# Wider recurrence products for the gates g, i and f, and q and k projections called by halves

## The reference, cut to what matters

```python
def step(carry, inp):
    h, c, n = carry
    i_t = sigmoid(xi_t + h @ Wih)
    f_t = sigmoid(xf_t + h @ Wfh)
    g_t = tanh(xg_t + h @ Wgh)
    o_t = sigmoid(xo_t + h @ Woh)
    c_t = f_t * c + i_t * g_t
    n_t = f_t * n + i_t * exp(g_t @ Weg + beg)
    h_t = o_t * (c_t / n_t)
...
qkv = x @ Wqkv          # per layer, q and k of 16 heads x 64
```

## Time and profile before

| | |
|---|---|
| median of 3 runs | 5900.19 us (5891.82 to 5912.33) |
| the profiled execution's own time | 5933.24 us |
| its span from first to last instruction | 5931.4 us |
| mean granted TensorE clock over the span | 0.895 |
| PE (matmul) busy | 5537.3 us, 93% |
| PEld (weight load) busy | 3641.9 us, 61% |
| DVE (VectorE) busy | 4517.5 us, 76% |
| ACT (ScalarE) busy | 2971.1 us, 50% |
| POOL (GpSimd) busy | 2368.6 us, 40% |

### The profile page before, as it was taken

One profiled execution on the slowest core, in us unless ns is written; L12 is line 12 of the kernel. 1 busy time (PEld: TensorE's weight loads), 2 busy tenths in 40 slices (PEclk: granted clock), 3 DMA queues, 4 the chain that ended last, 5 costly groups with the idle time before them and its releaser, 6 DMA issues. The chain is left out here.

```text
span 5931.4 us, 142026 instructions
## 1 busy us (share of the span) xinstructions
PE 5537.3 (93%) x51507; PEld 3641.9 (61%) x51508; DVE 4517.5 (76%) x15132; ACT 2971.1 (50%) x7179; POOL 2368.6 (40%) x2224
## 2 busy tenths in 40 slices
PE   4999999999999999999999999999998999998777
PEld 2555555666677666666666666667666555554353
DVE  4888888777777777787677677677777888886737
ACT  2666666444455454444444444454444666665030
POOL 3666665333333333333233333333333666664000
PEclk9999999888889899888788788898888999999888
DMA  3111110000000000000000000000001000000000
GB/s 111 32 35 35 35 39 21 17 16 14 16 14 16 14 25 5 25 12 12 5 25 5 24 5 25 5 25 5 25 5 30 28 28 28 28 11 1 10 2 17
DMA packets 106581, 123.24 MB, mean 21 GB/s; under 512 B 55014, under 2 KB 87480, under 8 KB 98872
## 3 DMA queue, kind: packets, MB, share of 16 engines
q1 hardware_dynamic: 105788, 114.34, 6.2%
q10 hardware_dynamic: 124, 0.03, 0.0%
HBM read 91.28 MB, written 23.07 MB: 19 GB/s over the span
## 5 line engine op out<-in xcount | busy, mean ns | idle before, releaser
L1593 POOL TENSOR_TENSOR t<-t 128x1024 f32<-128x1024 f32 x192 | 453.4, 2362 | 1264.3 <-DVE t L942 1264.3
L518 PE MATMUL banks<-h,lent 128*128 128x2 f32 x6144 | 937.3, 269 | 0.5 <-DVE banks L891 0.4
L594 PE MATMUL banks<-Wvo,xq 128*32 128x512 f32 x6144 | 891.7, 654 | 6.0 <-ACT Vw L1296 2.0
L518 PEld LDWEIGHTS banks<-h,lent 128*128 128x128 f32 x6144 | 884.6, 217 | 1.6 <-DVE banks L891 0.6
L1586 POOL TENSOR_TENSOR t<-t 128x1024 f32<-128x1024 f32 x192 | 453.9, 2364 | 868.5 <-DVE t L942 868.5
L515 PEld LDWEIGHTS banks<-h,lent 128*128 128x128 f32 x2048 | 373.1, 216 | 541.2 <-DVE h L923 403.6
L1219 ACT ACTIVATE ge<-banks 128x2 f32<-128x2 f32 x1024 | 176.1, 172 | 1001.6 <-PE banks L515 997.3
L910 DVE TENSOR_SCALAR banks<-es 128x6 f32<-128x6 f32 x1024 | 170.3, 166 | 634.5 <-ACT es L1228 625.3
L1296 ACT COPY Vw<-banks 128x512 f32<-128x512 f32 x768 | 450.9, 587 | 370.8 <-PE banks L594 364.7
L937 DVE TENSOR_TENSOR t<-banks,rl 128x1024 f32<-128x1024 f32 x384 | 468.5, 1220 | 106.9 <-ACT sq L1251 64.3
L1601 POOL TENSOR_TENSOR t<-t,rnorm 128x1024 f32<-128x1024 f32 x192 | 365.9, 1906 | 388.6 <-DVE rnorm L111 381.8
(11 more groups left out here) (314 smaller groups left out, 10820.1 us busy)
## 6 DMA issues: line engine op xcount, KB each, us to landing
Wqk<-in_L_ffn_Wqkv SPq DMA_DIRECT2D x24, 1024.0 KB, 5.0
Wvo<-wvo_kept SPq DMA_DIRECT2D x18, 1024.0 KB, 5.0
rl<-tables SPq DMA_DIRECT2D x24, 512.0 KB, 3.7
W<-in_L_ffn_W SPq DMA_DIRECT2D x24, 341.0 KB
tables<-tables SPq DMA_DIRECT2D x6, 1024.0 KB
wvo_kept<-Wvo SPq DMA_DIRECT2D x6, 1024.0 KB, 5.2
v_kept<-Vw SPq DMA_DIRECT2D x24, 256.0 KB, 2.5
Vw<-v_kept SPq DMA_DIRECT2D x24, 256.0 KB, 2.6
```

Source lines behind the costliest of these rows:

```text
L518: last = pe.matmul(sb[:, to + gate * B:to + (gate + 1) * B], c.Wg[:, gate + 1, 1, :], h, start=False, stop=True, skip_group_check=True)
L594: last = pe.matmul(vp[WIN * hq:WIN * hq + WIN, :], c.xq[n % 4][:, WIN * w:WIN * w + WIN], c.Wvo[stage % 2][:, hq, :], start=True, stop=True)
L1593: pool.tensor_tensor(t1, t1, t2[:, :], ALU.add).then_inc(s.k_sum, 1)
```

## The change

Three things change.

1. Each of the gates g, i and f takes h not once (2 columns) but repeated up to 32 times (64 columns). The last two columns of the output are the ones that the token needs; the others fall on the columns of tokens that have been used already, going backwards in the ring at its pitch of 4 or 6 columns, so nothing reads them. How often h is repeated follows from how many places lie behind the token in the bank: at the first token of a ring's first half 25 times for g and 17 for i and f, and 32 times from the eighth and the sixteenth token on and in the whole second half. To make this room, the rings begin at column 96 (`INPUTS`), and VectorE's scratch moves from column 384 to 480. Gate o and the product with Weg keep their two columns.
2. `project_q` and `project_k` do one half of the product at a call, and are called twice in a row at the same places; each half raises the semaphore. Nothing stands between the two calls.
3. The waits for `q_done` and `k_done` count twice as far.

```diff
+INPUTS, BROAD = 96, 32
-SUMS, SIGMAS, IG, RN = 384, 392, 400, 408
+SUMS, SIGMAS, IG, RN = 480, 488, 496, 504
...
+    def gate_of(k):
+        j, r = divmod(k, AHEAD)
+        return INPUTS + j % 2 * 4 * AHEAD + 4 * r, min(BROAD, r + 1 + INPUTS // 4 + j % 2 * AHEAD)
+
+    def sigmoids_of(k):
+        j, r = divmod(k, AHEAD)
+        return INPUTS + j % 2 * 6 * AHEAD + 6 * r, min(BROAD, r + 1 + INPUTS // 6 + j % 2 * AHEAD)
+
+    def ending(out, at, wide, n, part):
+        return out[:, at + wide - n * wide:at + wide].rearrange("p (n c) -> p n c", c=wide)[:, :, part * B:(part + 1) * B]
+
     def recur(k):
...
-        h = c.h[t % 2][:, :, i - 1] if i else c.h[1 - t % 2][:, :, P - 1]
-        at, to = j % 2 * 4 * AHEAD + 4 * r, j % 2 * 6 * AHEAD + 6 * r
+        h = (c.h[t % 2][:, :, i - 1] if i else c.h[1 - t % 2][:, :, P - 1]).unsqueeze(1)
+        (at, m), (to, n) = gate_of(k), sigmoids_of(k)
...
-        pe.matmul(ge[:, at:at + B], c.Wg[:, 0, 1, :], h, start=False, stop=True, skip_group_check=True).then_inc(s.g_done, 1)
+        pe.matmul(ending(ge, at, 4, m, 0), c.Wg[:, 0, 1, :], h.to_broadcast([P, m, B]), start=False, stop=True, skip_group_check=True).then_inc(s.g_done, 1)
...
         for gate in range(3):
-            last = pe.matmul(sb[:, to + gate * B:to + (gate + 1) * B], c.Wg[:, gate + 1, 1, :], h, start=False, stop=True, skip_group_check=True)
+            wide = n if gate < 2 else 1
+            last = pe.matmul(ending(sb, to, 6, wide, gate), c.Wg[:, gate + 1, 1, :], h.to_broadcast([P, wide, B]), start=False, stop=True, skip_group_check=True)
...
-    def project_k(n):
+    def project_k(n, h):
...
-        claim("qk", s.k_prod, 2 * n + 2)
-        for h in range(2):
-            last = pe.matmul(qk[h], c.xq[n % 4][:, :], c.Wqk[stage % 2][:, INNER + h * 512:INNER + (h + 1) * 512], start=True, stop=True)
-        last.then_inc(s.k_done, 1)
+        if h == 0:
+            claim("qk", s.k_prod, 2 * n + 2)
+        pe.matmul(qk[h], c.xq[n % 4][:, :], c.Wqk[stage % 2][:, INNER + h * 512:INNER + (h + 1) * 512], start=True, stop=True).then_inc(s.k_done, 1)
...
-        project_k(i - 2)
+        project_k(i - 2, 0)
+        project_k(i - 2, 1)
...
-        act.wait_ge(s.k_done, n + 1)
+        act.wait_ge(s.k_done, 2 * n + 2)
...
-                sp.wait_ge(s.k_done, 2 * SPAN * (stage - 1))
+                sp.wait_ge(s.k_done, 4 * SPAN * (stage - 1))
```

More of the change, by code:

```diff
@@ L521, in recur, with project_q @@
         pe.matmul(ge[:, at + B:at + 2 * B], c.Weg[:, :], c.ge[:, 0, :], start=False, stop=True, skip_group_check=True).then_inc(s.e_done, 1)
-    def project_q(n):
+    def project_q(n, h):
         if not tile_ok(n):
@@ L526, in project_q @@
         stage = place(n)[0]
-        pe.wait_ge(s.weights_in[stage % 2], 16 * (stage // 2 + 1))
-        pe.wait_ge(s.xq_ready, SHIFTS[n])
-        claim("qk", s.q_prod, 2 * n + 2)
-        for h in range(2):
-            last = pe.matmul(qk[h], c.xq[n % 4][:, :], c.Wqk[stage % 2][:, h * 512:(h + 1) * 512], start=True, stop=True)
-        last.then_inc(s.q_done, 1)
-    def project_k(n):
+        if h == 0:
+            pe.wait_ge(s.weights_in[stage % 2], 16 * (stage // 2 + 1))
+            pe.wait_ge(s.xq_ready, SHIFTS[n])
+            claim("qk", s.q_prod, 2 * n + 2)
+        pe.matmul(qk[h], c.xq[n % 4][:, :], c.Wqk[stage % 2][:, h * 512:(h + 1) * 512], start=True, stop=True).then_inc(s.q_done, 1)
+    def project_k(n, h):
         if not tile_ok(n):
@@ L833, in tensor_program @@
         turn_probs(i - 4, 0)
-        project_q(i - 1)
+        project_q(i - 1, 0)
+        project_q(i - 1, 1)
         attend(i - 4, 0)
@@ L847, in tensor_program @@
         b_rows(f - 1)
-        project_k(i - 1)
+        project_k(i - 1, 0)
+        project_k(i - 1, 1)
         step()
@@ L864, in tensor_program @@
         turn_k(i - 2, 1)
-        project_q(i)
+        project_q(i, 0)
+        project_q(i, 1)
         step()
@@ L890, in fill @@
         dve.wait_ge(s.evacuated, 4 * (t + 1))
-        dve.tensor_copy(d[:, j % 2 * 6 * AHEAD:(j % 2 + 1) * 6 * AHEAD],
+        dve.tensor_copy(d[:, INPUTS + j % 2 * 6 * AHEAD:INPUTS + (j % 2 + 1) * 6 * AHEAD],
                         c.vs[t % 2][:, part * 6 * AHEAD:(part + 1) * 6 * AHEAD]).then_inc(s.sb_filled, 1)
@@ L1210, in fill @@
         act.wait_ge(s.evacuated, 4 * (t + 1))
-        act.copy(ge[:, j % 2 * 4 * AHEAD:(j % 2 + 1) * 4 * AHEAD],
+        act.copy(ge[:, INPUTS + j % 2 * 4 * AHEAD:INPUTS + (j % 2 + 1) * 4 * AHEAD],
                  c.vg[t % 2][:, part * 4 * AHEAD:(part + 1) * 4 * AHEAD]).then_inc(s.ge_filled, 1)
@@ L1216, in recur_g @@
             return
-        at = k // AHEAD % 2 * 4 * AHEAD + 4 * (k % AHEAD)
+        at = INPUTS + k // AHEAD % 2 * 4 * AHEAD + 4 * (k % AHEAD)
         act.wait_ge(s.g_done, k + 1)
@@ L1225, in recur @@
         j, r = divmod(k, AHEAD)
-        at, to = j % 2 * 4 * AHEAD + 4 * r, j % 2 * 6 * AHEAD + 6 * r
+        at, to = INPUTS + j % 2 * 4 * AHEAD + 4 * r, INPUTS + j % 2 * 6 * AHEAD + 6 * r
         act.wait_ge(s.s_done, k + 1)
@@ L1239, in square_q @@
             return
-        act.wait_ge(s.q_done, n + 1)
+        act.wait_ge(s.q_done, 2 * n + 2)
         if n:
```

## The result

The changed kernel takes 5568.08 us, the median of 4 runs (5562.31 to 5574.25), against 5903.93 us for the kernel before (4 runs, 5891.82 to 5912.33): a ratio of 0.9433 (0.9411 to 0.9455). The forecast of 5480 us was 88 us too low; its wide range (5400 to 5700) holds the time, and so does the likeliest case's own range (5400 to 5570), by 2 us. The profiled execution took 5563.28 us, with a span of 5561.5 us and a mean granted clock of 0.963.

What follows compares the result with a forecast made beforehand. PE, busy throughout but partly at 1.2 GHz in the recurrence, was taken as the bound: profiled 5933 us less 431 for the clock, other parts 0, gives 5502; two thirds of a 33 us excess off gives 5480, range 5400 to 5700.

Steps and rivals of the forecast that it cites:

- the likeliest case: In the recurrence, the added columns hold most of the clock: 5480 us, own range 5400 to 5570, chance 0.62.
- The halves, the moved columns and the wider matmuls at zero: q and k by halves, buffers at other columns, and 6 x 1024 wider matmuls behind weight loads: each costed at 0.
- The 56 ns by which tanh might come later: In each step, the sum for tanh comes at most 56 ns later; 0.3 us of slack before L521 hides it.
- 479 us for the full clock: Largest possible gain if the clock stayed at 2.4 GHz through the whole recurrence: 479 us.
- 1066 us times 0.449: Recurrence time at 1.2 GHz, 1066 us, times 0.449 us lost per microsecond there, taken from two iterations.
- The share of nine tenths: Part of the 479 us clock gain in the recurrence expected to come: 431 us, a judgement.
- Both reasons given for the missing tenth: Fewer columns at first tokens of each ring's first half (25 and 17 pairs); steps where PE waits longer for VectorE.
- the step from the recording to the median: Profiled execution lay 33 us above the median; two thirds taken off, from 5502 to 5480 us.
- Half of the falls staying: Rival: in the poorest steps the clock needs more than the added columns; gain 240, some 5670 us, chance 0.11.
- no effect at all: Rival: the added columns don't hold the clock in the recurrence, nothing changes; 5900 us, chance 0.06.
- Slow streaming: Rival: alternating columns in g, i, f stream slowly; slower from 190 ns a matmul, 6110 us at 224 ns, chance 0.10.
- VectorE as a bound: Rival: VectorE, 85% busy, holds the recurrence's iterations at about 66 us; some 5575 us, chance 0.11.

Runs made afterwards that it cites:

- first two experiments: Changed kernel with columns back to 2, rest as changed: 5897.75 us; changed kernel with project_q and project_k whole again, columns as changed: 5565.98 us.
- the last kernel: Changed kernel with up to 128 columns in g, i, f and Weg's product, plus added matmuls in PE's waits for the y and b norms: 5525.52 us.
- 128 columns and the filled waits: Changed kernel with up to 128 columns in g, i and f, plus added matmuls in PE's waits for the y and b norms: 5534.58 us.

## Why the prediction came out as it did

*What held.* The mechanism: the gain is the clock's, all of it in the recurrence, and the columns alone bring it (first two experiments). The halves, the moved columns and the wider matmuls at zero: the six products keep their pace of 112 ns, at 64 and at 128 columns. (The prediction's 108 ns for two columns took off a mean of 269 ns over both levels of the clock; the starts themselves are 112 ns apart there too.) The 56 ns by which tanh might come later were 51 (over the full-clock steps the lower quartile went from 319 to 370 ns after g), and the slack of the earlier trace rows hid them: exp's start stayed at 988 and 1090 ns. The step with a projection, 2.94 us, was forecast at some 3. An iteration was forecast at 63.1 us in the mean; the mean is 65.2 us (3177.86 x 21/1023), and an ordinary one takes 62.2.

*The term that was mis-sized: 479 us for the full clock.* It was 1066 us times 0.449, a slope between two iterations, both ordinary ones. With the clock full throughout, the recurrence takes 3144 us, so the most that could go was some 3553 - 3144 = 409 us, perhaps 10 to 20 more, for the ordinary iterations of that kernel are 0.2 to 0.4 us longer than the changed kernel's. The forecast floor was 3074 us; 48.7 ordinary iterations of 62.3 us would even lie 39 us below that (3035). But in the last kernel some 109 us stand over this: 62 in the seven iterations with the norms that run whole in the recurrence (498.2 - 7 x 62.3), 29 in six others between 66.5 and 68.0 us, the rest spread. In those with the norms PE waits for VectorE at either clock, and so a microsecond at the lower level was worth less than 0.449 there. By the clock's records these seven held 181 of the 1044 us before and gave back 45 in the last kernel, 0.25 us for each; all the others held 864 and gave back 365, or 0.42. So of the 70 us that are missing, some 37 are those of the norms, 23 those of the others, and 10 come from a clock rounded to 0.85 (1066 us for 1044). I had read two iterations that were alike and applied their price to all 48.7.

*The share of nine tenths.* It was a judgement, and 375 of 409 us is 0.92. Both reasons given for the missing tenth are in the trace of the changed kernel. Of its 20 falls, 13 lie in the iterations in which PE waits for VectorE's norms. Of the other seven, four come at one of the first eight tokens of a ring's first half, an eighth of all tokens; with 128 columns and the filled waits it is four of six. That the few columns there cause them is likely, but not tested by itself.

*The sum again, with what was measured.* The profiled execution of the changed kernel took 5563, 61 us more than the 5502 of the forecast: 62.7 from the smaller maximum (0.9 x 69.7), less 7.1 for the larger share, and 5.6 for the rest of the span. The other 27 us are the step from the recording to the median. I took 22 us off, because the recording of the kernel before lay 33 above its median; that of the kernel after lies 5 below its own. I had also counted the excess as time at 1.2 GHz that the change removes; as the 431 us were worked out from that same recording, it was in them already, and taking it off again was the error. Together they make the 88 us.

*The rivals.* Half of the falls staying and no effect at all did not come. Slow streaming is refuted: with 128 columns, twice those of the change, the starts still lie 99 to 112 ns apart, where 190 was the point of decision. The page "SBUF — State Buffer" of the Trainium skill, "Specifications (TRN2)", let one expect a penalty when each column lies on a new 16-byte line; no run here shows one for TensorE's moving operand. VectorE as a bound is right only in the iterations with the norms: elsewhere it is 86% busy (53.71 of 62.21 us) and the iteration still has its steps of 2.7 us. That rival's time, 5575 us, came nearer to the measured one than the forecast did, but it had the iterations held at 66 us; their median is 62.4.

*What makes the clock fall.* The page "TensorE: Matmul & The Clock Gate" of the Trainium skill, section "Why this matters for your kernels", ties falls to idle gaps. In the iterations with the norms the traces agree: a wait of 3.32 us, a fall behind it, and a clock of 1.00 once the wait is filled. For the other falls they don't: in the kernel with four narrow steps an iteration, PE's longest wait in the step of a fall and the two before it is under 0.5 us at 41 of the 42 falls outside those iterations, and PE is busy 96% of the recurrence (3254.50 of 3392.18 us, the row below). And the number of columns alone takes the falls from 96 to 20, although PE is idle no less (137 us of the recurrence with 2 columns, 169 us with 64). My own refinement, that the falls' places decide, failed: widening the poor steps alone brought 71 us, widening all others 125. What in a stretch decides over a fall, beyond that, these runs leave open.

The window of the recurrence of that kernel, whose steps 10 to 13 are narrow:

```profile
1008.09:4400.27 3392.18, 3254.50 (x30448) 2330.58 (x30446) 2691.21 (x11239) 1689.38 (x5114) 1188.43 (x1094) 0.90 0.05 16
```

## What to carry to other kernels

Where PE is busy and its granted clock is still below full, look at how much its matmuls stream, not only at its gaps: 62 more columns in six of a step's ten matmuls, behind weight loads that are paid anyway, were worth 6% here, and 14 more only 1%. Price time at the lower clock by the longest and the oddest iterations too, since a wait on another engine bounds what the clock can give back. And a wait of PE for a chain of another engine's small operations can be worth filling, even with work that nobody reads: here it cost once as a wait and again in the slow steps behind it.

## What was not expected of the hardware

A moving operand whose two columns lie 512 bytes apart and alternate 64 times went at the pace of contiguous columns. A wide matmul behind which a narrow one follows lets that one start early: with 64 columns, o's second product starts 84 ns after its first where 112 stood, and 59 ns with 128; the six products are over no later than narrow ones. And the gains from the clock do not add up: two sets of steps that bring 71 and 125 us alone bring 336 together.
